# A residual sum moved from GpSimd to VectorE and a skip product moved on TensorE, in a chunked selective scan

## The reference, cut to what matters

```python
xn = layernorm(x, in_norm_alpha, in_norm_bias)
x_in, z = split(xn @ in_proj_w.T + in_proj_b)
x_conv = silu(causal_conv(x_in, 4 taps) + conv_b)
Bm, Cm = split(x_conv @ x_proj_w.T + x_proj_b)
delta = clip(softplus(x_conv @ dt_proj_w.T + dt_proj_b), 1e-4, 10)
h = exp(clip(delta * A, -10, 0)) * h + delta * Bm * x_conv   # per token; every 16th one bounds the norm of h
y = (Cm . h + D_param * x_conv) * silu(z)
out = layernorm(residual + y @ out_proj_w.T + out_proj_b, norm_alpha, norm_bias)
x = x + out                                                  # the sum that the change moves
```

## Time and profile before

| what | value |
|---|---|
| median of 3 runs | 4293.99 us |
| profiled execution: own time, span | 4292.5 us, 4290.7 us |
| busy share of the span: TensorE, VectorE, ScalarE, GpSimd | 92%, 79%, 72%, 62% |
| mean granted TensorE clock | 0.988 |
| scan stage, attention stage | to about 2830 us, from there to the end |
| skip product (L779), `x1` (L416), clamp (L1253) | 64 times each |

### The profile page before, as it was taken

One profiled execution on the slowest core, in us unless ns is written; L12 is line 12 of the kernel. 1 busy time (PEld: TensorE's weight loads), 2 busy tenths in 40 slices (PEclk: granted clock), 3 DMA queues, 4 the chain that ended last, 5 costly groups with the idle time before them and its releaser, 6 DMA issues. The chain is left out here.

```text
span 4290.7 us, 72241 instructions
## 1 busy us (share of the span) xinstructions
PE 3927.4 (92%) x19008; PEld 2537.1 (59%) x19008; DVE 3404.5 (79%) x7970; ACT 3069.2 (72%) x9040; POOL 2644.6 (62%) x1412
## 2 busy tenths in 40 slices
PE   5798989898989898989898989779999999999999
PEld 5666666666666666666666666534545445454454
DVE  3799999999999999999999999845766667666666
ACT  6999999999999999999999999734333332333321
POOL 3999999999999999999999999910000000000000
PEclk8899999999999999999999999989999999999999
DMA  2111111111111212121111111100000000000000
GB/s 108 61 53 65 52 65 52 65 52 65 52 65 52 64 53 64 54 63 56 61 56 60 59 58 61 49 26 24 8 15 17 7 17 7 16 17 7 7 7 10
DMA packets 91266, 187.60 MB, mean 44 GB/s; under 512 B 15872, under 2 KB 57600, under 8 KB 90624
## 3 DMA queue, kind: packets, MB, share of 16 engines
q1 hardware_dynamic: 91136, 186.11, 13.1%
HBM read 168.24 MB, written 17.83 MB: 43 GB/s over the span
## 5 line engine op out<-in xcount | busy, mean ns | idle before, releaser
L768 PE MATMUL ps<-w_x,mxT 128*128 128x512 f32 x4096 | 1936.6, 601 | 105.4 <-DVE macc L1120 105.4
L1120 DVE SCALAR_TENSOR_TENSOR macc<-ps,gate,macc 128x256 f32<-128x256 f32 x2048 | 980.2, 479 | 507.0 <-PE ps L768 421.1
L1027 DVE TENSOR_TENSOR_SCAN hb<-ps_dA,hb 128x1088 f32<-128x1088 f32 x512 | 1240.7, 2423 | 56.7 <-issue 5.5
L396 POOL TENSOR_TENSOR hb<-u,bbc 128x1024 f32<-128x1024 f32 x512 | 1203.6, 2351 | 84.2 <-issue 38.1
L449 ACT ACTIVATE zr<-dt,aneg 128x128 f32<-128x128 f32 x4096 | 1246.1, 388 | 0.1
L365 POOL TENSOR_TENSOR prod<-hb,cbc 128x1024 f32<-128x1024 f32 (+2 forms) x640 | 1192.8, 1869 | 18.4 <-DVE hb L1027 13.4
L768 PEld LDWEIGHTS ps<-w_x,mxT 128*128 128x128 f32 x4096 | 722.4, 190 | 791.4 <-issue 588.9
L734 PE MATMUL ps<-ident,prod 128*128 128x128 f32 x4096 | 503.1, 277 | 67.2 <-POOL prod L365 64.8
L734 PEld LDWEIGHTS ps<-ident,prod 128*128 128x128 f32 x4096 | 456.1, 142 | 171.9 <-POOL prod L365 87.4
L458 ACT ACTIVATE ps_dA<-zr 128x1024 f32<-128x1024 f32 x512 | 517.9, 1012 | 0.0
L511 ACT ACTIVATE ex<-lgt,ms 128x16 f32<-128x16 f32 x128 | 39.4, 307 | 361.5 <-DVE ms L1068 361.5
(11 more groups left out here) (204 smaller groups left out, 4682.3 us busy)
## 6 DMA issues: line engine op xcount, KB each, us to landing
bbc<-bcd SPq DMA_DIRECT2D x128, 512.0 KB, 3.7
cbc<-bcd SPq DMA_DIRECT2D x128, 512.0 KB, 3.8
xt<-in_x SPq DMA_DIRECT2D x128, 128.0 KB, 2.9
x2d<-macc SPq DMA_DIRECT2D x64, 128.0 KB, 1.7
out_dram<-macc SPq DMA_DIRECT2D x64, 128.0 KB, 1.7
w_x<-in_w_x SPq DMA_DIRECT2D x1, 4096.0 KB, 15.6
hb<-x2d SPq DMA_DIRECT2D x32, 128.0 KB, 2.3
sz<-x2d SPq DMA_DIRECT2D x16, 128.0 KB, 2.2
```

The source lines that it names most:

```text
L396: TT(hb[c % 2][:].rearrange("p (e n) s -> p e n s", e=EB)[:, :, :, 1:SL], u[k][:, :, t0:t0 + CH].rearrange("p e (n s) -> p e n s", n=1).br ...
L768: last = mm(banks[p % len(banks)][:], mxT[k][:, j, :], w_x[:, j, p * 512:(p + 1) * 512], start=(j == 0), stop=(j == KD - 1))
L1027: V.tensor_tensor_scan(states, dA, states, 0.0, ALU.mult, ALU.add).then_inc(M["scan"], 1)
L1120: STT(macc[k][:], banks[(e // 2) % len(banks)][:, (e % 2) * D:(e % 2 + 1) * D], gate[k][:, e:e + 1], macc[k][:], ALU.mult, ALU.add).then_i ...
```

## The change

The residual sum `x1` leaves GpSimd's chunk 7 and becomes an addition on VectorE in chunk 4, which reads `closing` in PSUM directly: `o4` is now written in place there, and the buffer `oo` is gone. The skip product goes from chunk 3 to behind z's product in chunk 4 and waits for `x1` in place of `o4`. The clamped convolution gets its own buffer `xc`, since the skip product of tile i still reads `xcv[k]` when the convolution of a later tile is clamped; GpSimd then writes `xcv[k]` from `xc` and waits for the skip product (a new semaphore `sk`). `yT` shrinks to one half that serves both copies. VectorE's idle increments at the start go from 72 to 57.

```diff
-        yT = sb("yT", [P, E])
+        yT = sb("yT", [P, D])
+        xc = sb("xc", [P, EB, P])
...
-        oo = sb("oo", [P, D])
...
                 if c == 5 and "F" in stages:
                     g.wait_ge(M["sx"], AHEAD + i + 3)
-                    TT(xcv[k][:], xcv[k][:], sg[:], ALU.mult).then_inc(M["xcv"], 1)
-                if c == 7 and "B" in stages:
-                    g.wait_ge(M["o4"], AHEAD + i)
-                    g.wait_ge(R["ac"], AHEAD + (i - 3) * (X + 1) + 1)
-                    TT(x1b[1 - k][:], oo[:], xt[1][:], ALU.add).then_inc(M["x1"], 1)
+                    g.wait_ge(M["sk"], AHEAD + (i + 1 if "S" in stages else 0))
+                    TT(xcv[k][:], xc[:], sg[:], ALU.mult).then_inc(M["xcv"], 1)
...
-                a.wait_ge(M["yb"], AHEAD + (i - 1) * 2 + half + 1)
-                act(yT[:, half * D:(half + 1) * D], YT[:, half * D:(half + 1) * D], ACT.Copy).then_inc(M["yt"], 1)
+                a.wait_ge(M["yb"], AHEAD + i * 2 + half)
+                act(yT[:], YT[:, half * D:(half + 1) * D], ACT.Copy).then_inc(M["yt"], 1)
...
-                        act(sg[:], xcv[k][:], ACT.Exp, scale=-1.0).then_inc(M["ex"], 1)
+                        act(sg[:], xc[:], ACT.Exp, scale=-1.0).then_inc(M["ex"], 1)
...
             def skip(i, k):
 
                 for e in range(EB):
-                    mm(YP[:].rearrange("p (t e) -> p e t", e=EB)[:, e, :], ddp[:, e, :], xcv[k][:, e, :], start=(e == 0),
-                       stop=False)
+                    last = mm(YP[:].rearrange("p (t e) -> p e t", e=EB)[:, e, :], ddp[:, e, :], xcv[k][:, e, :], start=(e == 0),
+                              stop=False)
+                last.then_inc(M["sk"], 1)
...
                     if c == 3 and S_:
                         sum_states(i, 0)
-                        pe.wait_ge(M["o4"], AHEAD + (i if B else 0))
-                        pe.wait_ge(M["xcv"], AHEAD + i + 1)
-                        skip(i, k)
...
                         last.then_inc(M["z"], 1)
+                    if c == 4 and S_:
+                        pe.wait_ge(M["x1"], AHEAD + (i if B else 0))
+                        pe.wait_ge(M["xcv"], AHEAD + i + 1)
+                        skip(i, k)
...
-                    v.wait_ge(M["x1"], AHEAD + i - 1)
-                    STT(oo[:], closing, sc[:, 12:13], be_row[:], ALU.mult, ALU.add).then_inc(M["o4"], 1)
+                    STT(closing, closing, sc[:, 12:13], be_row[:], ALU.mult, ALU.add).then_inc(M["o4"], 1)
...
                 router(2, 3)
+                if B:
+                    v.wait_ge(M["o4"], AHEAD + i)
+                    v.wait_ge(R["ac"], AHEAD + (i - 3) * (X + 1) + 1)
+                    TT(x1b[1 - k][:], closing, xt[1][:], ALU.add).then_inc(M["x1"], 1)
...
                 if F:
                     v.wait_ge(M["conv"], AHEAD + i + 3)
-                    TS(xcv[k][:], bank4(F0), -40.0, None, ALU.max).then_inc(M["xcc"], 1)
+                    v.wait_ge(M["xcv"], AHEAD + i + 2)
+                    TS(xc[:], bank4(F0), -40.0, None, ALU.max).then_inc(M["xcc"], 1)
...
-            for _ in range(72):
+            for _ in range(57):
                 settle()
```

More of the change, by code:

```diff
@@ L169, in build @@
         dve_m = ("st1", "mv1", "vp", "den", "sx1", "nx", "keep", "xib", "zb", "xcc", "bcv", "dtb", "scan", "nr",
-                 "st0", "hs", "yg", "o2", "st3", "mv3", "vc3", "se3", "r3", "o3", "o4")
+                 "st0", "hs", "yg", "o2", "st3", "mv3", "vc3", "se3", "r3", "o3", "o4", "x1")
         act_m = ("xn", "carry", "lnp", "r1", "qs", "xnTs", "ez", "lz", "ss", "ex", "lx", "sx", "edt", "ldt", "zr", "dA", "sq", "nl",
                  "ne", "ln3", "sd3", "yt")
-        pool_m = ("sz", "xcv", "u", "bt", "prodp", "x1")
-        pe_m = ("xnT", "xi", "z", "conv", "bc", "dtp", "y", "yb", "op")
+        pool_m = ("sz", "xcv", "u", "bt", "prodp")
+        pe_m = ("sk", "xnT", "xi", "z", "conv", "bc", "dtp", "y", "yb", "op")
         sp_m = ("x", "xr", "bcd", "bb0", "bb1", "cc0", "cc1")
@@ L741, in sums_back @@
                 for h in (2 * half, 2 * half + 1):
-                    last = mm(YP[:, h * P:(h + 1) * P], yT[:, h * P:(h + 1) * P], ident[:], start=False, stop=(h == 3),
+                    last = mm(YP[:, h * P:(h + 1) * P], yT[:, h % 2 * P:(h % 2 + 1) * P], ident[:], start=False, stop=(h == 3),
                               is_transpose=True)
@@ L804, in step @@
                             pe.wait_ge(M["dtb"], AHEAD + NTILES)
-                            pe.wait_ge(M["o4"], AHEAD + NTILES)
+                            pe.wait_ge(M["x1"], AHEAD + NTILES)
                         transposes(early_tile(i, c, 1))
```

## The result

The changed kernel takes 4376.26 us (median of four runs, 4376.12 to 4376.89), the kernel before 4294.16 us beside it: a ratio of 1.019 [1.0177, 1.0204]. That is 16 us over the predicted 4360 and inside the range. The profiled execution took 4376.12 us, its span is 83.6 us longer than that of before, and its mean granted clock is 0.979.

A forecast was written before the change was run, and what follows sets the result against it. The step was taken to close over VectorE's chunk 3 expert sum and TensorE's work up to the chunk 7 experts. 4292.5 + 31 (dense stretch) + 37 (clock) - 2 = 4358.5, so 4360 us as median; range 4312 to 4400.

The forecast's parts named there:

- The mechanism: TensorE's scan steps: a longer dense stretch, and a clock lost behind 2.4 us of idle time in chunk 3; chance 0.50.
- The sum on VectorE: Chunk 4: the addition takes 0.40 us and fills the clamp's 0.43 us wait for the convolution, so it costs 0.
- GpSimd's relief: Chunk 7: taking 0.74 us of work off GpSimd gains 0, bounds 0 and 0.74 us per step.
- the faster case: Rival: GpSimd is the pace, so 0.74 us less work in chunk 7 shortens each step; 4250 or 4272 us; chance 0.12.
- The skip product behind z: TensorE's dense stretch: 0.87 us of matmuls less slack and refill, +0.57 us even, +0.47 odd, mean +0.52, 31 us in all.
- the slack before the projection: TensorE's B/C projection waiting for GpSimd's `xcv`: 0.10 us of slack in even steps and 0.30 us in odd ones.
- refill: TensorE's refill after a wait: 0.10 us, saved when the projection's wait for `xcv` goes.
- The clock: TensorE behind chunk 3's idle time: half clock in three of four of 29 even steps, 1.7 us each, 37 us.
- The rest: Fewer idle increments at the start, -1.3 us, and `x1` off GpSimd's path in the last steps, -0.7 us; -2 us together.
- The clock holds: Rival: the dense stretch gets longer but the 2.4 us gap leaves the clock at 1.00; 4323 us; chance 0.22.
- Both kinds of step lose it: Rival: odd steps' chunk 3 gap also grows enough to lose the clock; 4397, up to 4410 us; chance 0.08.
- Hidden: Rival: the skip product fits into TensorE's slack before the projection, as weight loads suggest; 4292 to 4298 us; chance 0.08.

The follow-up runs named there:

- the first experiment: The kernel before with only the residual sum moved to VectorE's chunk 4, both operands in SBUF: 4356.03 us, ratio 1.0146.
- the filled run: The changed kernel with eight useless matmuls in TensorE's chunk 3, behind the state sums, to shorten its idle time: 4333.5 us, ratio 1.0093.
- the run with the lengthened stretch: The changed kernel with eight useless matmuls in TensorE's chunk 3 idle time and eight more behind the skip product: 4386.65 us, ratio 1.0214.

## Why the prediction was right, and where it was off

- **The mechanism held.** The skip product left a place where TensorE waited and went into a stretch that sets the end of chunk 7; TensorE's idle time in chunk 3 grew to about the forecast 2.4 us (2.33 in the row above, 1.54 before); the clock fell there in even steps only. VectorE's wait for the chunk 7 experts rose by 0.78 us, nearly the 0.75 us by which the dense stretch grew. Filling that idle time gives back 42.8 us, which shows the clock's share.
- **The sum on VectorE: 0, right.** It takes 0.41 us, forecast 0.40, and fills the wait for the convolution; the run with the skip product alone is as slow without it. That it would be free hung on a point that I did not weigh: with both operands in SBUF it cost 62 us in the first experiment.
- **GpSimd's relief: 0, right.** The run with the sum alone in PSUM shows it. The rival by which GpSimd was the pace falls, and with it the faster case.
- **The skip product behind z: +0.52 us a step forecast, 0.75 measured.** This is the term that was mis-sized, and the step that failed is the slack before the projection. I set "where four such matmuls with work behind them need 1.72 us" against the 1.82 us of the even step and called 0.10 us slack. The changed kernel has no wait there and the distance is still 1.82 us (1419.74 to 1421.56), and 1.81 in the odd step. The 1.72 us came from a row in which another kind of matmul follows, and does not carry over to the projection. The projection's weight load says the same: its idle time is 0.76 us in the changed kernel, where it waits for nothing that the profile shows, and was 0.76 in the even step before and 0.96 in the odd one. So there was no slack in the even step and 0.2 us in the odd one. These are the load in the changed kernel's even step, and then in the even and the odd step before:

```profile
1421.55 0.79 PEld L874 LDWEIGHTS ps<-xcv,w_xp 128*32 128x32 f32 x8 [0.76 <-issue]
...
1470.99 0.79 PEld L875 LDWEIGHTS ps<-xcv,w_xp 128*32 128x32 f32 x8 [0.76 <-POOL xcv L412]
...
1427.84 0.79 PEld L875 LDWEIGHTS ps<-xcv,w_xp 128*32 128x32 f32 x8 [0.96 <-POOL xcv L412]
```

Nor was there a refill to win: the projection's 0.99 us to the next work (1421.56 to 1422.55) is what it was, 1471.00 to 1471.99 in the trace before:

```profile
1471.99 0.39 PE L774 MATMUL ps<-split 128*128 128x512 bf16 x1
```

Put right, the odd step is 0.90 - (2.02 - 1.81) = 0.69 us, measured 0.67. The even step is 0.90 less what the experts' start gained in chunk 3: they follow VectorE's sum by 0.06 us in place of 0.20, and take 0.10 us more behind the wait, which leaves 0.04; that makes 0.86 us, measured 0.84. By the measured values that makes 44.5 us over 59 steps, for the forecast 31.

- **The clock: 37 us forecast, 43.7 measured.** The price of one loss was about right, 1.62 us for 1.7. The count was not: 27 of 29 even steps, forecast three in four from the four idle stretches of the earlier trace rows. In the loop the steps repeat (a pair takes 88.74 us, and the losses lie that far apart), and after the first loss, in step 8, every even step up to 60 had one; the last steps, which differ from one another, were a poor sample for that. Since what decides on a loss is open (see the last section), it is in part luck that three in four came so near.
- **The rest: -2 us forecast, -3.8 measured.** VectorE's idle time ahead of its first `xin` is 4.93 us for the 6.32 of the earlier trace rows, as forecast, but tile 3 begins 3.4 us earlier. Where the other 2 us of the start come from was not followed. One reading was wrong without weight: "42.6 us (2000/47)" counts waits in a window and is no step; the steps before take 42.63 us even and 43.00 us odd.

```profile
22.10 0.69 DVE L1239 TENSOR_TENSOR xin<-ps,b_in 128x512 f32<-128x512 f32 x1 [4.93 <-issue]
```

- **The other rivals.** The clock holds: the forecast 4323 us would have been about 4334, as the filled run shows. Both kinds of step lose it: the odd idle time grew to 1.79 us and stayed harmless. Hidden: the projection's weight load had 0.0 and 0.2 us of slack, as said above, and the run with the lengthened stretch shows 0.90 us of cost for 0.90 us of work.

The prediction weighed a sentence of the Trainium skill (TensorE: Matmul & The Clock Gate, section "HAM oscillation — how this bites in real kernels") by which only longer gaps than these would let the clock fall. The trace differs: in the even steps 8 to 58 the clock fell behind idle stretches of 2.33 to 2.39 us, and in step 60 behind one of 2.06 us. The measurement decides.

## What to carry to other kernels

An operation that stands in a wait is free there; before it is moved, find the stretch that it goes to, and ask whether that has a wait at all. A distance between two instructions is slack only if the same two instructions are seen closer together elsewhere. Where an engine's idle time grows, look at the clock behind it, and at what releases the engine: moving the releasing instruction ahead of work whose result is needed only later, here the expert sum ahead of the layernorm's end, took off all that the change had cost.

## What was not expected of the hardware

**An addition on VectorE with both operands in SBUF, beside a busy GpSimd, is four times as long.** The same 128x256 addition took 1.81 us on average in the first experiment and 0.41 with one operand in PSUM. In the attention stage, where GpSimd does nothing, one with both operands in SBUF takes 0.425 us, as this group by line of the kernel before shows:

```profile
L1420 DVE TENSOR_TENSOR bbc<-bbc,hb 128x256 f32<-128x256 f32 x32 | 13.6, 425 | 1.1
```

In the first experiment it ended 0.26 to 0.28 us behind the end of the GpSimd instruction that ran when it began, in each of the 63 steps that had one, though it took from 0.56 to 2.05 us. The last one, with no GpSimd instruction beside it, took 0.42 us:

```profile
2878.07 0.42 DVE L1247 TENSOR_TENSOR x1b<-oo,xt 128x256 f32<-128x256 f32 x1
```

So what grew is a wait for GpSimd's instruction to end. The Trainium skill (GPSIMD Engine Reference, section "1. Specifications") lists VectorE instructions with two SBUF inputs among those that contend with GpSimd for SBUF; this case agrees and gives the size.

**A loss of the clock can repeat with the loop, and the length of the idle time alone does not decide on it.** From step 8 to step 60 each even step of the changed kernel lost the clock. Step 6 had 2.41 us of idle time and kept it. Step 60 had only 2.06 us and lost it, while the odd step behind it kept it with 2.05 us (its experts took 1.98 us). The first two:

```profile
342.93 1.98 PE L765 MATMUL ps<-w_x,mxT 128*128 128x512 f32 x4 [2.41 <-DVE macc L1119]
...
2736.99 3.57 PE L765 MATMUL ps<-w_x,mxT 128*128 128x512 f32 x4 [2.06 <-DVE macc L1119]
```

What else decides was not tried here.
